# Macaron block with mixture-of-experts and attention: maxima and results turned through DRAM, first norm in two parts

## The chip, the cores and the metric

The kernel runs on one core of a Trainium2 chip. The metric is the time of one execution on the device, in microseconds (us). One core has TensorE (PE; the weight loads are shown apart as PEld), VectorE (DVE), ScalarE (ACT), GpSimd (POOL) and SyncE (SP), each with a queue of its own, and 16 DMA engines that are fed from such queues.

## What is computed

x has 4 sequences of 1024 tokens of 128 numbers, in float32. The layer is a half-weighted expert network, attention, and the same expert network again:

```python
x = x + 0.5 * ffn(layernorm(x), W1, b1, W2, b2, Wr, br)
x = x + attn(layernorm(x), Wq, bq, Wk, bk, Wv, bv, Wo, bo)
x = x + 0.5 * ffn(layernorm(x), W1, b1, W2, b2, Wr, br)

def ffn(x, ...):
    indices = argmax(softmax(x @ Wr + br))
    for i in range(8):
        xi = x * (indices == i)
        out = out + (relu(xi @ W1[i] + b1[i]) @ W2[i] + b2[i])

def attn(x, ...):
    q, k, v = (x @ W + b, split into 16 heads of 8 numbers)
    scores = einsum('bhsd,bhtd->bhst', q, k) / sqrt(8)
    return merge(einsum('bhst,bhtd->bhsd', softmax(scores), v)) @ Wo + bo
```

A token that is not expert i's still gets relu(b1[i]) @ W2[i] + b2[i] from it. These rows are the same for all tokens; the kernel calls them idle and adds their sum to the one expert's result.

## The kernel before

The tokens are 32 tiles of 128, in 8 quads of 4 tiles. There are three stages, and each block of engine programs ends with all engines meeting.

**Routing** (`route`, L253 to L482) normalises x, turns it, takes the logits, finds each token's place among the tokens sorted by expert, and writes a list of source rows. `Norm` makes statistics (L63, L74), a root on ScalarE (L83), scales on VectorE (L77, L89 to L97) and applies them (L102). In the first routing, `Setup` also loads all inputs, fills constant rows of the attention's buffers with memsets on GpSimd (L182 to L187), takes the idle rows with 64 products (L203), and sums them up on VectorE (`vector_idle` L225, `vector_rest` L233 to L237, the latter called from `list_items`, ahead of L711). The marks (L378, L380) and the columns (L382) are one-hot matrices from which TensorE makes the list (L461).

**The experts** (`Tiles`, L485 to L768) gather sorted rows with indirect DMAs on GpSimd (L559), run 39 items of a tile and an expert, and scatter the result (L566).

**Attention** (`attention`) begins with a prologue that normalises, projects, and splits q and k into three bf16 parts, stored in DRAM (L924, L936) and read back as rows (`load_heads`, L906 to L911). It goes by 16 groups of 4 heads of one batch. A group has 32 maxima units in two halves of 16. A unit is two pairs of products of queries with keys in the bank pair `ps_m` (L1071) and a maximum on VectorE (L1287). Softmax takes the row's maximum away inside the score product: two guard rows of q2 hold its negative, split into two bf16 parts, and so must be there before the half's scores. A group has 16 steps; a step has four score products (L1114), four exponentials on ScalarE (L1269), and the value products (L1125, eight records a step), whose weights have columns of ones, so that the sums come out beside the results. Those of half a group collect in one bank `ps_o`, which ScalarE copies to `oT` (`take_out`, L1190).

The order of the units is written out in `schedule`, and each takes the next of the two bank pairs of `ps_m` (`slot_of`):

```python
pair = [("max", u) for u in range(AHEAD + 2 * s, AHEAD + 2 * s + 2) if u < GROUPS * P1_UNITS]
head, tail = pair, []
if k == 3 and g:
    head, tail = pair[0:1] + [("o", g - 1)], pair[1:2]
if (s + 4) % KT == 0 and (s + 4) // KT < HALVES:
    head, tail = [("m", (s + 4) // KT)] + pair[0:1], pair[1:2]
```

TensorE does a step's head units, three scores, its tail unit, the value products of the step before and the fourth score; VectorE does its part of the units in the same order. Four kinds of unit are not maxima. An `m` unit turns a half's combined maxima (L1295) on TensorE (L1077), ScalarE and VectorE split them (L1196, L1305), and SP places them with eight DMAs (`place_guard`, L986). An `o` unit turns a group's results with 8 transposes (L1083); VectorE inverts the sums (L1312) and multiplies (L1314). For a quad of results, a `c` unit turns the gathered rows (L949, L1099, L1330) and a `y` unit multiplies by Wo (L1105); VectorE adds bo and x (L1338, L1341). Six quads (`MERGED`) are done in the last steps, two behind them (`FINISH`), while VectorE applies the second routing's norm to the six. SP's queue, in order, has the prologue's stores, the first guards ahead of the last two stores, a wait for all stores, group 1's loads, and then by group: loads for the group after next, guards of the odd half, guards of the next group's first half.

## Time and profile before

| | us |
|---|---|
| median of 3 runs (lowest to highest) | 1068.44 (1066.82 to 1069.05) |
| the profiled execution | 1066.93 |
| its span, first to last instruction | 1065.0 |
| TensorE busy, share of the span | 943.2, 89% |
| VectorE busy | 857.1, 80% |
| ScalarE busy | 741.8, 70% |
| GpSimd busy | 182.3, 17% |

The times are of the whole program. The profile is of one execution, whose time is 1.93 us longer than its span. A share of busy time is an average over the stages; matmuls are pipelined, so that a busy TensorE is not TensorE at its peak. The mean granted clock of TensorE was 0.953 of full speed.

### The profile page before, as it was taken

Reading aid. Unit: us, or ns where it says so; the run is one execution under the profiler, and the core shown is the slowest. Engines: PE = TensorE matmul, PEld = TensorE weight load, DVE = VectorE, ACT = ScalarE, POOL = GpSimd, SP = SyncE. Lnnn points to the kernel's source line nnn. Section 1 sums busy time; section 2 is a strip of 40 time slices with the busy share of each in tenths; the row PEclk is TensorE's granted clock in tenths of the full one; section 3 lists DMA queues with packets and bytes.
Section 4 is the critical chain, followed back from the end, with each engine's and each line's share of the span. In section 5 each row is a group of like instructions: output and inputs, shape, how many; then the busy total and the mean of one; then the engine's idle time right before and its main releaser. Section 6 shows DMA issues by size and latency. Waiting matters only on the chain. (4 is left out here: it accounts for less than half of the span.)

```text
span 1065.0 us, 18032 instructions
## 1 busy us (share of the span) xinstructions
PE 943.2 (89%) x6037; PEld 389.0 (37%) x6037; DVE 857.1 (80%) x1459; ACT 741.8 (70%) x1493; POOL 182.3 (17%) x198
## 2 busy tenths in 40 slices
PE   0769956779999999999999999999999999953996
PEld 0569942312222222222222222222222223442996
DVE  6876668958888888888888888888888886568664
ACT  0147726758878788787887878878788787821774
POOL 7077623700000000000000000000000000002775
PEclk9969978989999999999999999999999999965999
DMA  8533136731120202202022020220202000032321
GB/s 269 162 90 90 45 108 225 243 99 32 46 45 1 46 1 46 45 1 46 1 46 46 2 45 1 46 45 1 45 2 46 1 2 1 1 112 73 107 68 41
DMA packets 60945, 63.20 MB, mean 59 GB/s; under 512 B 8152, under 2 KB 46968, under 8 KB 60856
## 3 DMA queue, kind: packets, MB, share of 16 engines
q1 hardware_dynamic: 54152, 48.53, 17.0%
q0 software_dynamic: 5120, 12.59, 3.9%
q8 instruction: 51, 0.84, 0.3%
q10 hardware_dynamic: 1584, 0.93, 0.3%
q14 instruction: 38, 0.31, 0.1%
HBM read 36.59 MB, written 25.17 MB: 58 GB/s over the span
## 5 line engine op out<-in xcount | busy, mean ns | idle before, releaser
L1269 ACT ACTIVATE probs<-ps_s 128x512 f32<-128x512 f32 x1024 | 556.3, 600 | 144.3 <-PE ps_s L1114 118.6
L1287 DVE TENSOR_REDUCE maxima<-ps_m 128x2 f32<-128x1024 f32 x512 | 600.7, 1217 | 60.6 <-PE ps_m L1071 59.9
L1114 PE MATMUL ps_s<-q,k 74*128 74x512 bf16 (+1 forms) x1024 | 313.2, 387 | 1.3 <-ACT probs L1269 1.2
L1125 PE MATMUL ps_o<-probs,vs 128*32 128x512 f32 x2048 | 273.9, 607 | 0.7 <-ACT probs L1269 0.7
L1114 PEld LDWEIGHTS ps_s<-q,k 74*128 74x128 bf16 (+1 forms) x1024 | 81.3, 97 | 310.7 <-ACT probs L1269 230.3
L1071 PE MATMUL ps_m<-k,q 64*128 64x512 bf16 x1024 | 172.7, 387 | 21.4 <-DVE maxima L1287 12.2
L1035 POOL COPY vs<-v_and_ctx 128x256 f32<-128x256 f32 x16 | 6.3, 400 | 583.2 <-PE ps_o L1125 583.2
L1071 PEld LDWEIGHTS ps_m<-k,q 64*128 64x128 bf16 x1024 | 46.6, 93 | 138.0 <-issue 57.6
L604 PE MATMUL ps_y<-W,hT 128*128 x624 | 83.5, 277 | 0.0
L559 POOL DMA_INDIRECT v_and_ctx<-token_rows,source_i x64 | 62.3, 974 | 112.5 <-POOLq L300 93.7
L1125 PEld LDWEIGHTS ps_o<-probs,vs 128*32 128x32 f32 x2048 | 40.4, 108 | 100.7 <-issue 75.1
L604 PEld LDWEIGHTS ps_y<-W,hT 128*128 128x128 f32 x624 | 76.7, 194 | 0.4 <-issue 0.4
L633 ACT ACTIVATE xsT<-ps_x 128x128 f32<-128x128 f32 x64 | 17.7, 277 | 74.7 <-PE ps_x L583 74.6
L642 ACT ACTIVATE w1s<-W 128x644 f32 x78 | 57.8, 743 | 5.8 <-DVE by_delta L711 4.8
L649 ACT ACTIVATE hT<-ps_ha,w1s 128x128 f32<-128x128 f32 x156 | 48.4, 365 | 10.0 <-PE ps_hb L592 10.0
L592 PE MATMUL ps_ha<-xsT,w1s 128*128 (+1 forms) x312 | 50.2, 285 | 4.4 <-ACT w1s L642 4.4
L751 DVE TENSOR_SCALAR hT<-ps_hb,w1s 128x128 f32<-128x128 f32 x156 | 47.6, 347 | 5.7 <-PE ps_hb L592 1.6
L592 PE MATMUL ps_hb<-xsT,w1s 128*128 (+1 forms) x312 | 49.2, 282 | 0.0
L592 PEld LDWEIGHTS ps_ha<-xsT,w1s 128*128 128x128 f32 x312 | 43.2, 200 | 5.0 <-issue 5.0
L763 DVE SCALAR_TENSOR_TENSOR v_and_ctx<-y_sum,half_mask,v_and_ctx 128x128 f32 x78 | 27.4, 352 | 20.7 <-DVE y_sum L758 20.7
L592 PEld LDWEIGHTS ps_hb<-xsT,w1s 128*128 128x128 f32 x312 | 42.8, 199 | 0.0
L758 DVE TENSOR_TENSOR y_sum<-ps_y,w1s 128x128 f32<-128x128 f32 x78 | 22.8, 292 | 24.8 <-PE ps_y L604 24.8
(171 smaller groups left out, 590.1 us busy)
## 6 DMA issues: line engine op xcount, KB each, us to landing
k_rows<-parts SPq DMA_DIRECT2D x24, 384.0 KB, 3.7
q<-q_parts SPq DMA_DIRECT2D x75, 96.0 KB
k<-k_rows SPq DMA_DIRECT2D x15, 288.0 KB
token_rows<-x SPq DMA_DIRECT2D x16, 256.0 KB, 4.0
token_rows<-v_and_ctx SPq DMA_DIRECT2D x16, 256.0 KB, 3.8
q<-mpart SPq DMA_DIRECT2D x256, 1.0 KB
k<-k_rows SPq DMA_DIRECT2D x15, 256.0 KB
q_parts<-parts SPq DMA_DIRECT2D x8, 384.0 KB, 3.5
```

The costliest lines, as they stand in the source:

```text
L559: nc.gpsimd.indirect_dma_start(self.xs[:, t, :], None, self.dram["token_rows"], bass.IndirectOffsetOnAxis(ap=self.routes.source_i[:, t:t + ...
L592: last = nc.tensor.matmul(self.ps_h[c // 2][i % 2][:, (c % 2) * P:(c % 2 + 1) * P], self.w1s[:, i % W_ROTATION, c * P:(c + 1) * P], self.x ...
L604: last = nc.tensor.matmul(self.ps_y[i % 2][:, 0:D], self.hT[:, i % 2, c * P:(c + 1) * P], w["W2"][:, bass.ds(e, 1), c, :].rearrange("p a d ...
L642: nc.scalar.activation(self.w1s[:, i % W_ROTATION, :], w["W1"][:, bass.ds(e, 1), :].rearrange("p a h -> p (a h)"), ACT.Copy).then_inc(self ...
L649: last = nc.scalar.activation(self.hT[:, i % 2, c * P:(c + 1) * P], self.ps_h[0][i % 2][:, c * P:(c + 1) * P], ACT.Relu, bias=self.w1s[:, ...
L751: last = nc.vector.tensor_scalar(self.hT[:, i % 2, c * P:(c + 1) * P], self.ps_h[1][i % 2][:, (c - 2) * P:(c - 1) * P], self.w1s[:, i % W_ ...
L763: nc.vector.scalar_tensor_tensor(out=row, in0=self.y_sum[:, i % 2, :], scalar=self.half_mask[:, i:i + 1], in1=row, op0=ALU.mult, op1=ALU.a ...
L1071: last = nc.tensor.matmul(ps_m[slot][:, j % 2, :], q2[buffer(g)][rows, j, qt * P:(qt + 1) * P], k2[buffer(g)][rows, j, kh * HALF:(kh + 1) ...
L1114: nc.tensor.matmul(ps_s[n % 3][:, :], k2[buffer(g)][0:contracted, j, kt * P:(kt + 1) * P], q2[buffer(g)][0:contracted, j, u * HALF:(u + 1) ...
L1125: last = nc.tensor.matmul(ps_o[32 * j:32 * (j + 1), :], vs[buffer(g)][:, kt, j, :], probs[:, s % 2, j, :], start=(kt == 0), stop=(kt == KT ...
L1269: nc.scalar.activation(probs[:, s % 2, j, :], ps_s[n % 3][:, :], ACT.Exp, scale=SCALE).then_inc(exped, 1)
L1287: nc.vector.tensor_reduce(maxima[:, :, pr, qt, kh], ps_m[slot][:, :, :], AX.X, ALU.max).then_inc(unit_free[slot], 1)
```

## The change

- **Maxima.** The `m` units are gone. VectorE combines a half's maxima as before; GpSimd splits them with three small operations (`split_maxima`); VectorE turns them in blocks of 32 x 32 (`turn_maxima`), one or two units later; SP stores them to DRAM (`guards`), waits, and reads them back as guard rows with two DMAs.
- **Results.** The `o` and `c` units are gone. SP stores each half group's `oT` in DRAM (`sums`), waits, and reads results and sums back in the layout in which TensorE takes them for Wo (`results`). VectorE inverts the sums of half a batch at once, 128 x 512 (`invert`), at the steps in `DIVIDED` (60, 71, 124, 135, 188, 199, 252; the eighth behind the last step); GpSimd multiplies (`multiply`; VectorE for the last). GpSimd adds bo to x early on (`add_bias`), and the `y` units only add to x. Seven quads are merged instead of six.
- **The end of the attention.** ScalarE and SP send the last results' rows straight from `oT` with four small DMAs each. ScalarE applies the norm to two of the seven quads, VectorE to five.
- **Loads.** Group 1's loads go out before the stores of quads 6 and 7, with the first guards behind them. The first loads of group 0 go out before the stores of quad 1, and the statistics and scales of the prologue's norm are spread among other work.
- **The first routing.** Its norm goes in two parts of four quads; ScalarE applies quads 0, 1, 4 and 6. Half of the marks goes to ScalarE, half to GpSimd (both routings). The idle rows are copied by ScalarE and summed on GpSimd (`add_up`, `gpsimd_rest`), and `RESTED` is waited for there.

```diff
-    def vector_idle(self, dve):
-        dve.wait_ge(self.idle_done, 1)
-        self.nc.vector.tensor_copy(self.idle[:, :, :], self.ps_idle[:, :, :]).then_inc(self.dve_step, 1)
...
+    def scalar_idle(self, act):
+        act.wait_ge(self.idle_done, 1)
+        self.nc.scalar.activation(self.idle[:, :, :], self.ps_idle[:, :, :], ACT.Copy).then_inc(self.idle_out, 1)
...
+    def add_up(self, pool, rows, out, before):
+
+        nc, tree, half = self.nc, self.tree, EXPERTS // 2
+        wait_unless_zero(pool, self.rest_step, before)
+        nc.gpsimd.tensor_tensor(tree[:, :, :], rows[:, 0:half, :], rows[:, half:, :], ALU.add).then_inc(self.rest_step, 1)
+        pool.wait_ge(self.rest_step, before + 1)
+        nc.gpsimd.tensor_tensor(tree[:, 0:2, :], tree[:, 0:2, :], tree[:, 2:4, :], ALU.add).then_inc(self.rest_step, 1)
+        pool.wait_ge(self.rest_step, before + 2)
+        nc.gpsimd.tensor_tensor(out[:, :], tree[:, 0, :], tree[:, 1, :], ALU.add).then_inc(self.rest_step, 1)
+
+    def gpsimd_biases(self, pool):
+
...
+    def gpsimd_rest(self, pool):
 
...
+        pool.wait_ge(self.idle_out, 1)
+        self.add_up(pool, self.idle, self.total, 3)
+        pool.wait_ge(self.rest_step, 6)
+        nc.gpsimd.tensor_tensor(self.total[:, :], self.total[:, :], self.biases[:, :], ALU.add).then_inc(self.rest_step, 1)
+        pool.wait_ge(self.rest_step, 7)
+        half = EXPERTS // 2
...
-                for q in range(ready, QUADS):
+                def statistics(q):
...
-                    last = norm.statistics(quad_tiles(q))
-                last.then_inc(vstep, 1)
-                norm.spread(dve, late)
-                norm.refine(dve, late)
-                for q in range(ready, QUADS):
-                    norm.apply(quad_tiles(q))
...
+                    norm.refine(dve, (span.start, span.stop), n)
+                    nc.vector.scalar_tensor_tensor(out=shift[:, span], in0=mv[:, span, 0], scalar=-1.0, in1=rt[:, 6, span],
+                                                   op0=ALU.mult, op1=ALU.mult).then_inc(shifted, 1)
+
+                for n, (first_quad, end_quad) in enumerate(spans):
+                    for q in range(first_quad + (n > 0), end_quad):
+                        last = statistics(q)
+                    last.then_inc(vstep, 1)
+                    norm.spread(dve, (first_quad * QUAD, end_quad * QUAD), n)
+                    if n + 1 < len(spans):
+                        statistics(end_quad)
+                    scales(n)
+                    for q in range(first_quad, end_quad):
+                        if q not in by_act:
+                            norm.apply(quad_tiles(q))
...
-                dve.wait_ge(routed, 22)
-                nc.vector.tensor_tensor(marks[:, :, 0, :], hot[:, :, :],
-                                        w["iota_b"][:, 0:TILES].unsqueeze(2).to_broadcast([P, TILES, TILES]), ALU.mult)
-                nc.vector.tensor_scalar(marks[:, :, 1, :], hot[:, :, :], w["partition"][:, 0:1], None, ALU.mult)
+                dve.wait_ge(routed, 21)
...
                     setup.gpsimd_fill(pool)
+                    setup.gpsimd_biases(pool)
+                pool.wait_ge(routed, 22)
+                nc.gpsimd.tensor_tensor(marks[:, :, 0, :], hot[:, :, :],
+                                        w["iota_b"][:, 0:TILES].unsqueeze(2).to_broadcast([P, TILES, TILES]), ALU.mult).then_inc(marked, 1)
...
+                def normalise(q):
+                    act.wait_ge(shifted, 1 if q < QUAD else 2)
+                    for t in quad_tiles(q):
+                        last = nc.scalar.activation(xn_sb[:, t, :], x_sb[:, t, :], ACT.Identity, bias=shift[:, t:t + 1], scale=rt[:, 6, t:t + 1])
...
+                act.wait_ge(routed, 22)
+                nc.scalar.activation(marks[:, :, 1, :], hot[:, :, :], ACT.Copy, scale=w["partition"][:, 0:1]).then_inc(marked, 1)
+                if setup:
...
+MERGED = 7
+OUTPUT_STEP = (243, 245, 247, 249, 251, 252, 254)
...
-    merged = {SOFT - 2 * MERGED - (n == 0) * 2 + n: [(("c", "y")[n % 2], n // 2)] for n in range(2 * MERGED)}
+    merged = {s: [("y", q)] for q, s in enumerate(OUTPUT_STEP)}
...
-        steps.append((head + merged.get(s, []), tail))
+        steps.append([("max", u) for u in range(AHEAD + 2 * s, AHEAD + 2 * s + 2) if u < GROUPS * P1_UNITS] + merged.get(s, []))
...
+
+    at = {}
+    for q in range(MERGED):
+        b, u = divmod(q, 2)
...
+        def last_results(engine, target, first):
+
+            engine.wait_ge(o_out, 2 * GROUPS)
+            for j in range(GH):
+                row = (GPB - 1) * GH * DK + j * DK
+                engine.dma_start(target[row:row + DK, :], oT[32 * j + first:32 * j + first + DK, 1, :]).then_inc(o_in[1], 16)
...
                 def place_guard(h):
...
+                    sp.wait_ge(turned_maxima, h + 1)
+                    sp.dma_start(dram["guards"][h, :, :].rearrange("c (a r) -> a c r", r=32), blocks[h % 2][:, :]).then_inc(guards_out, 16)
+                    sp.wait_ge(guards_out, 16 * (h + 1))
...
+                    for j in range(2):
+                        sp.dma_start(q2[buffer(g)][guard(j):guard(j) + GUARDS, j::2, u * HALF:(u + 1) * HALF], rows[j, :, :, :]).then_inc(in_m[buffer(g)], 16)
...
+                def results(g, u):
...
+                    sp.wait_ge(o_out, 2 * g + u + 1)
+                    sp.dma_start(dram["sums"][g, u, :, :], oT[:, u, :]).then_inc(o_stored[u], 16)
+                    sp.wait_ge(o_stored[u], 16 * (g + 1))
+                    if g % GPB == 0 and b:
+                        sp.wait_ge(divided, 2 * b - 1 + u)
+                    sp.dma_start(ctxT[rows, tokens], sums[:, 0:DK, :]).then_inc(o_in[u], 16)
+                    sp.dma_start(den[rows, u, :], sums[:, DK:2 * DK, :]).then_inc(o_in[u], 16)
...
                 store(0)
-                store_key(sp, 1, 0)
-                store_query(sp, 1)
                 first_load(0)
-                store_key(sp, 1, 1)
-                store_key(sp, 1, 2)
+                store(1)
                 first_load(1)
-                for q in range(FIRST, QUADS - 2):
+                for q in range(FIRST, QUADS):
+                    if q == QUADS - 2:
+                        place_guard(0)
                     store(q)
-                place_guard(0)
-                for q in range(QUADS - 2, QUADS):
-                    store(q)
+                    if q == QUADS - 3:
+                        load(1)
                 for p in range(2):
                     sp.wait_ge(parts_stored[p], 16 * STORES * (QUADS // 2))
-                load(1)
                 for g in range(GROUPS):
                     if 1 <= g < GROUPS - 2:
                         sp.wait_ge(step_done, STEPS * g)
                         load(g + 2)
+                    if g:
+                        results(g - 1, 1)
                     place_guard(2 * g + 1)
                     if g == 0:
                         load(2)
+                    results(g, 0)
                     if g + 1 < GROUPS:
                         place_guard(2 * g + 2)
+                last_results(sp, ctxT[:, (QUADS - 1) * HALF:], 0)
                 for p in range(BUFS):
-                    sp.wait_ge(in_m[p], 16 * 2 * GH * GUARDS * ((GROUPS - 1 - p) // BUFS + 1))
+                    sp.wait_ge(in_m[p], 16 * 2 * 2 * ((GROUPS - 1 - p) // BUFS + 1))
+                for u in range(2):
+                    sp.wait_ge(o_in[u], O_IN * GROUPS + (2 * GH * 16 - O_IN if u else 0))
...
+                def split_maxima(h):
+
+                    pool.wait_ge(combined, h + 1)
+                    wait_unless_zero(pool, turned_maxima, h)
+                    nc.gpsimd.tensor_scalar(split[:, :, 0, :], top[:, :, :], -1.0, None, ALU.mult).then_inc(split_step, 1)
+                    nc.gpsimd.tensor_scalar(negated[:, :, :], top[:, :, :], -1.0, None, ALU.mult).then_inc(split_step, 1)
+                    pool.wait_ge(split_step, 3 * h + 2)
+                    nc.gpsimd.tensor_tensor(split[:, :, 1, :], negated[:, :, :], split[:, :, 0, :], ALU.subtract).then_inc(split_step, 1)
...
+                def multiply(q):
+
+                    pool.wait_ge(recip, q + 1)
+                    columns = ctxT[:, q * HALF:(q + 1) * HALF]
+                    nc.gpsimd.tensor_tensor(columns, columns, den[:, q % 2, :], ALU.mult).then_inc(divided, 1)
...
-                for q in range(MERGED):
-                    gather_rows(pool, nc.gpsimd.tensor_copy, q)
+                split_maxima(1)
+                for q in range(QUADS):
+                    add_bias(q)
+                split_maxima(2)
+                for g in range(1, GROUPS):
+                    if g < GROUPS - 2:
+                        pool.wait_ge(step_done, STEPS * g)
+                        stage(g + 2)
+                    if g % GPB == 0:
+                        split_maxima(2 * g + 1)
+                        multiply(2 * (g // GPB) - 1)
+                    else:
+                        split_maxima(2 * g + 1)
+                    if g + 1 < GROUPS:
+                        split_maxima(2 * g + 2)
+                    if g % GPB == GPB - 1:
+                        multiply(2 * (g // GPB))
 
             @block.tensor
...
+                    wait_unless_zero(act, o_stored[u], 16 * g)
...
-                    gather_rows(act, nc.scalar.copy, q)
+                last_results(act, den[:, 1, :], DK)
+                act.wait_ge(shifted_2, 1)
+                for t in range(BY_DVE, MERGED * QUAD):
+                    last = nc.scalar.activation(xn_next[:, t, :], w["x"][:, t, :], ACT.Identity, bias=shift[:, t:t + 1], scale=rt[:, 6, t:t + 1])
+                last.then_inc(normed_2, 1)
 
...
-
-                def split_unit(h, slot, used):
-
-                    dve.wait_ge(unit_full[slot], used + 1)
...
-                    nc.vector.tensor_tensor(ctx_sb[:, g, :, :].rearrange("p t (j d) -> p t j d", d=DK),
-                                            src[:, :, :, 0:DK], rden[:, :, :, :].to_broadcast([P, KT, GH, DK]),
-                                            ALU.mult).then_inc(unit_free[slot], 1)
+                    nc.vector.tensor_reduce(top[:, :, :].rearrange("p a (i t) -> p a i t", t=QUAD), maxima[:, :, :, u:u + QUAD, :],
+                                            AX.X, ALU.max).then_inc(combined, 1)
+
+                def turn_maxima(h):
+
+                    dve.wait_ge(split_step, 3 * h + 3)
+                    if h >= 2:
+                        dve.wait_ge(guards_out, 16 * (h - 1))
+                    nc.vector.transpose(blocks[h % 2][:, :], split[:, :, :, :].rearrange("p a r c -> p (a r c)")).then_inc(turned_maxima, 1)
+
+                def invert(q):
+
+                    b, u = divmod(q, 2)
+                    dve.wait_ge(o_in[u], O_IN * GPB * (b + 1) + (2 * GH * 16 - O_IN if q == QUADS - 1 else 0))
+                    nc.vector.reciprocal(den[:, u, :], den[:, u, :]).then_inc(recip, 1)
...
+                    nc.vector.tensor_tensor(w["x"][:, tiles_of, :], ps_m[slot][:, 0, :].rearrange("p (t d) -> p t d", d=D), w["x"][:, tiles_of, :],
+                                            ALU.add).then_inc(unit_free[slot], 1)
                     if q < MERGED:
-                        dve.wait_ge(residual, q + 1)
+                        dve.wait_ge(unit_free[slot], used + 1)
...
+                norm_2.apply(range(BEFORE_LAST))
+                invert(QUADS - 1)
+                dve.wait_ge(recip, QUADS)
+                columns = ctxT[:, (QUADS - 1) * HALF:]
+                nc.vector.tensor_tensor(columns, columns, den[:, 1, :], ALU.mult).then_inc(divided, 1)
+                norm_2.apply(range(BEFORE_LAST, BY_DVE))
+                for unit in FINISH:
                     do_unit(*unit)
-                for q in range(len(FINISH) - 1, MERGED):
-                    norm_2.apply(quad_tiles(q))
+
 
```

## Rows read from the trace of the kernel before

**Rows 1.** Busy time by stage (stretch, length, engines with instructions, clock, DMA share, GB/s)

```profile
267.20:888.40 621.20, 613.87 (x3725) 157.97 (x3724) 545.88 (x533) 501.37 (x953) 5.92 (x14) 1.00 0.12 26
...
888.40:930.30 41.90, 39.96 (x271) 16.77 (x270) 24.03 (x70) 32.90 (x62) 2.45 (x4) 1.00 0.01 1
...
930.30:947.10 16.80, 7.12 (x36) 5.88 (x32) 12.49 (x44) 3.24 (x5) 0.00 (x0) 0.59 0.00 0
```

**Rows 2.** Timeline of TensorE in one group (start, us, line, instructions merged)

```profile
400.30 1.06 PE L1125 MATMUL ps_o<-probs,vs 128*32 128x512 f32 x8
...
402.92 1.07 PE L1125 MATMUL ps_o<-probs,vs 128*32 128x512 f32 x8
...
406.56 1.06 PE L1125 MATMUL ps_o<-probs,vs 128*32 128x512 f32 x8
...
409.48 1.06 PE L1125 MATMUL ps_o<-probs,vs 128*32 128x512 f32 x8
...
411.43 0.39 PE L1071 MATMUL ps_m<-k,q 64*128 64x512 bf16 x2 [0.23 <-DVE maxima L1287]
...
412.50 1.06 PE L1125 MATMUL ps_o<-probs,vs 128*32 128x512 f32 x8
```

**Rows 3.** Timeline of VectorE in the same stretch (in brackets: idle before, and what ended it)

```profile
402.05 2.36 DVE L1287 TENSOR_REDUCE maxima<-ps_m 128x2 f32<-128x1024 f32 x2 [0.27 <-PE ps_m L1071]
...
408.83 0.28 DVE L1305 SCALAR_TENSOR_TENSOR mpart<-ps_m,mpart 16x128 bf16<-16x128 f32 x1 [0.93 <-ACT mpart L1196]
```

**Rows 4.** Timeline of TensorE at the start of the softmax

```profile
218.94 1.06 PE L1125 MATMUL ps_o<-probs,vs 128*32 128x512 f32 x8
...
225.62 1.04 PE L1071 MATMUL ps_m<-k,q 64*128 64x512 bf16 x4 [5.29 <-DMA q<-q_parts]
...
231.99 1.07 PE L1125 MATMUL ps_o<-probs,vs 128*32 128x512 f32 x8
```

**Rows 5.** Groups by line and shape, VectorE (count, busy us, mean ns, idle before)

```profile
L89 DVE RECIPROCAL rt_a<-rt_a 128x4 f32<-128x4 f32 x2 | 0.4, 178 | 0.8 <-ACT rt_a L83 0.8
...
L89 DVE RECIPROCAL rt_a<-rt_a 128x24 f32<-128x24 f32 x1 | 0.3, 291 | 0.0
...
L89 DVE RECIPROCAL rt<-rt 128x32 f32<-128x32 f32 x1 | 0.4, 355 | 0.3 <-ACT rt L83 0.3
...
L1341 DVE TENSOR_TENSOR x<-x,plus_bo 128x512 f32<-128x512 f32 x8 | 5.5, 692 | 0.3
...
L77 DVE TENSOR_SCALAR rt_a<-mv_a 128x24 f32<-128x24 f32 x1 | 0.2, 178 | 0.0
```

**Rows 6.** Timeline of SP's queue

```profile
200.05 5.74 SPq L986 DMA_DIRECT2D q<-mpart  x8
...
398.80 0.31 SPq L906 DMA_DIRECT2D k<-k_rows  x1
...
402.87 0.30 SPq L911 DMA_DIRECT2D q<-q_parts  x1
```

**Rows 7.** DMA issues (count, KB each, median us from issue to landing)

```profile
token_rows<-x SPq DMA_DIRECT2D x16, 256.0 KB, 4.0
...
b_rows<-L_ffn_b SPq DMA_DIRECT2D x1, 16.0 KB, 1.8
```

**Rows 8.** Groups by line and shape, GpSimd

```profile
L959 POOL TENSOR_TENSOR probs<-probs,parts 128x512 f32<-128x512 f32 x12 | 13.7, 1154 | 30.1 <-ACT parts L1218 30.1
```

**Rows 9.** Timeline of VectorE and GpSimd in the first norm

```profile
19.12 1.80 POOL L183 MEMSET k<- 64x2048 bf16 x1
...
19.47 1.49 DVE L77 TENSOR_SCALAR rt<-mv 128x32 f32<-128x32 f32 x1
...
20.98 1.80 POOL L185 MEMSET q<- 64x2048 bf16 x1
...
22.09 0.72 DVE L95 TENSOR_SCALAR rt<-rt 128x32 f32<-128x32 f32 x1
```

**Rows 10.** Timeline of ScalarE at the first weights

```profile
62.95 0.74 ACT L642 ACTIVATE w1s<-W 128x644 f32 x1 [4.45 <-DVE by_delta L711]
```

255 lines of the change are left out of this document (111 added, 144 removed).

## The prediction

> **What bounds the kernel now.** I read the busy time by stage first [rows 1]. The softmax stage from 267.2 to 888.4 is 621.2 us long, with TensorE busy for 613.87 of it, VectorE for 545.88 and ScalarE for 501.37; the granted clock is 1.00, the 2.4 GHz level. So TensorE's queue sets the pace there, and VectorE is not far behind. The timeline of TensorE [rows 2] shows how. The starts of the value products (L1125) mark the steps. A plain step is 402.92 - 400.30 = 2.62 us. The step with the turn of the results (L1083) takes 406.56 - 402.92 = 3.64, so that unit costs 1.02. The steps on which a turn of the maxima (L1077) bears take 409.48 - 406.56 = 2.92 and 412.50 - 409.48 = 3.02, so that unit costs 0.30 + 0.40 = 0.70; the second part is the stop at 411.43, where TensorE waits for VectorE, which had stood 0.93 us behind ScalarE's part of the split [rows 3]. VectorE in a plain step has 0.27 us to spare. Early on, a stop of 5.29 us waits for group 1's loads [rows 4]. Outside the softmax, the routing stages and the turn between softmax and routing are chains of small dependent pieces.
>
> **Softmax, units taken out.** The pattern stands in all sixteen groups. Between 267.2 and 888.4 and in the group before, 30 turns of maxima and 14 turns of results go (the last of each falls into the end, below): 30 x 0.70 + 14 x 1.02 = 35.3 us less on TensorE, which no other engine hides. The work put in their place is on GpSimd (three small operations a half), SP (three DMAs a half instead of eight, and three more for the results) and VectorE (one 32-column transpose a half, near 0.2 us as the reciprocal and other 32-column rows are). GpSimd is idle there, and the transpose fits into VectorE's 0.27 us: I cost both at nothing. If that cover were gone, the transposes would be worth 31 x 0.2 = 6 us.
>
> **Softmax, the new reciprocals.** Before, a reciprocal had 32 columns. Now eight have 512 columns of 128 partitions, and six of them stand between maxima in VectorE's queue (steps 60, 71, 124, 135, 188, 199). The trace has 178 ns for 4 columns and 355 for 32 [rows 5]: 6.3 ns a column, so 178 + 508 x 6.3 = 3.4 us. From below, it might go like an addition of the same shape, 0.69 us [rows 5]; from above, the slope between 24 and 32 columns is 8.0 ns, which would make it 4.2 us. I take 3.4, as the rows are of this very operation and the longer distance smooths them. Behind it the maxima wait, behind them TensorE, which has two banks for them: it loses 3.4 less the spare 0.27, 3.1 us, six times: +18.6. 
>
> **The early stall.** From 218.94 to 231.99 two steps take 13.05 us [rows 4]; without the wait they would take 2 x 2.62 + 0.30 = 5.54. Group 1's loads now go out before the last two stores, 5 us or more earlier than needed: -7.5. They are put ahead of the first guard rows on SP, though. Before, these went out at 200.05 [rows 6] and nothing waited for them. Now SP sends ten loads first (398.80 to 403.17 in a later group, 4.4 us [rows 6]), then a store to DRAM, a wait for it, and two loads. A small transfer lands in 1.8 us, one of 256 KB in 4.0 [rows 7]. So: 200 + 4.4 + 0.5 + 2.5 + 0.7 + 2.0 = 210.1, and TensorE's first unit of the softmax, at 209.7 before, comes out at 210.4: +0.7. The first norm's rearrangement in this block wins some 2 us on VectorE ahead of that (statistics put into its waits, the first maxima begin earlier), and the guard wait eats them. Bounds: -2 and +4.
>
> **The end of the softmax.** From 888.4 to 930.3 [rows 1] seven y units stand where six pairs of c and y, one o and one m stood. That wins about 1.6 us, but the seventh reciprocal (step 252) is followed by a multiplication on GpSimd (1.15 us for this shape [rows 8]) and the y unit at step 254: 3.4 + 1.2 after VectorE comes to it, about 2.3 us too late for TensorE. Net +0.7, bounds -2 and +4.
>
> **The tail.** It is 16.8 us long now [rows 1], a chain through all engines. The new one: 0.6 for the copy out of the bank, four DMA issues 1.8, landing 2.0, reciprocal 3.4, multiplication 0.7, Wo at the low clock 2.1, addition 0.7, and gaps, 11.7 in all; the norm of the other tiles runs beside it. -5.1.
>
> **The first routing.** The clue is here [rows 9]. A VectorE scale operation on 32 columns (L77) took 1.49 us and ended at 20.96, as the memset begun at 19.12 for 1.80 us had just ended; L95 took 0.72 and ended at 22.81, as the memset begun at 20.98 had ended. L77 on 24 columns takes 178 ns [rows 5]. So such operations stand still while GpSimd works. The change moves the norm of quads 0 to 3 into the time of the memsets, which last until 23.8 us. Ten such operations there (two of the scales, eight applications) get through only at the memsets' ends, one or two at each, so the last of them ends between 21 and 24 us, and the statistics of quads 5 to 7 (2.6 us), which are queued behind them, then their scales (3.3) and ScalarE's eight applications (3.2, at 0.4 each) end at 30 to 33 us, where VectorE had ended all at 31.6; ScalarE's copies then stand behind its applications, 6 us to the logits where it was 4.3. So splitting the norm, which without the blocking would bring the logits 4.5 us forward, brings nothing; I take +1.0. Then the marks on GpSimd (1024 columns, 2.3 us by [rows 8]) and the rest of the sums (5.2 us) meet the 32 column operations (5.3 us), which are of the same blocked kind and now wait where they ran back to back; the block can't end before GpSimd's sums, which follow TensorE's 64 products and ScalarE's copy of them: another +4. Against that, VectorE's sums ahead of the first weights go (ScalarE waits 4.45 us for them [rows 10]), and with their gaps the first products start 4.6 us sooner after the block: -4.6. Sum +0.4; bounds -8.2 (nothing is blocked) and +6. The Trainium skill (SBUF — State Buffer, SBUF: two separate sides) calls the port pair that VectorE and GpSimd share an exclusive lock, held for the full instruction. By that rule, this part of the change is hurt as above; the trace agrees, with its 1.49 us. In the second routing, a norm of four tiles instead of eight wins 0.8 and the marks on GpSimd lose 0.8: nothing.
>
> **New waits.** VectorE waits for GpSimd's split before each transpose, with maxima behind it; two units (2.4 us) lie between, so it is hidden but for the first, 1 to 1.5 us, in the prologue (within the bounds there). SP waits for each store of sums and of guards; behind it are the next loads. For an odd half: the loads are issued 2.9 us after the group's first value product, the sums land behind them at 8.9 (0.4 + 4.0 and 1.6 for the loads still moving), their reads are issued by 9.9, the guards' two trips end at 15.1 (0.4 + 2.0 + 0.8 + 2.0), and TensorE needs them at 17.1, 1.2 ahead of seven plain steps. ScalarE's wait for the sums stored a group before is long met.
>
> **The sum** is against the profiled execution, 1066.9 us: -35.3 + 18.6 - 7.5 + 0.7 + 0.7 - 5.1 + 0.4 = -27.5, so 1039.4. The median of the runs is 1.5 above that execution: 1040.9.
>
> **Rivals.** (1) GpSimd and VectorE don't block each other as the first routing supposes, because the loser gets in between two operations cheaply. For it: a GpSimd memset began 20 ns after L77 ended, unharmed. Against: 1.49 and 0.72 us. Then first routing -8.2 instead of +0.4, second -2.4 instead of 0: 1029.9. Chance 0.2. (2) The long reciprocal costs like an addition. Six times 2.7, 2.7 in the tail and 2.3 in the end less: 1019.7. Chance 0.08. (3) The early stall doesn't go, as the loads still land behind the stores, or guards take its place: 1048.4. Chance 0.1. (4) Slower: the guard rows come late in each odd half. Their way now has two trips through DRAM in a row behind the sums. If each trip takes the 4.0 us of the larger stores instead of 2.0 [rows 7], the 4.0 more less the 2.0 to spare leave 2.0 late, and 2.7 with 0.7 of issue time: 15 groups x 2.7 = 40 us, 1081. It decides from about 1.8 us a group on. Against it: the guards are 8 KB. Chance 0.1. The forecast's own case has 0.5, and 0.02 is for a stall that just cancels the gain.
>
> **Numbers.** The range takes in cases 1, 2 and 3 and the bounds of the main one (1028 to 1056, the reciprocal of 4.2 us, 6 us more, among them): 1018 to 1057, leaving out rival 4 and a little more. A measurement of this kernel can tell about 0.2% from no change. Faster by more than that has 0.9, within it 0.02, slower 0.08.
>
> **What would show it.** Right: plain steps still of 2.62 us in all places where L1083 and L1077 stood; six gaps of 3 us in the steps behind the reciprocals, each of them 3.4 us long; the stop at group 1's loads gone; scale operations of the first norm lasting to the ends of memsets; the block behind the softmax over some 12 us after the last value product. Wrong: TensorE waits for guard rows at the half's first step, or reciprocals under 1 us, or logits of the first routing well before 35 us.

## The result, and the profile after

The changed kernel takes 1057.61 us (median of 5 runs, 1053.53 to 1058.40), the kernel before 1067.74 us beside it: a ratio of 0.9896 with the 95% interval 0.9884 to 0.9909, so 10 us or 1% faster. The forecast was 1040.9 us with a range up to 1057: the sign was right, and the gain was 10 us where 27.5 were forecast. The profiled execution has a span of 1055.5 us against 1065.0.

The page of the changed kernel, its busy times and the row of the granted clock:

```profile
span 1055.5 us, 17569 instructions
PE 912.6 (86%) x5771; PEld 371.6 (35%) x5845; DVE 857.0 (81%) x1397; ACT 747.9 (71%) x1488; POOL 230.9 (22%) x314
PEclk9779978979999988999999899999989999965999
```

TensorE's busy time is 30.6 us less than before (943.2 there). Part of that is a gap in the page: it has records of 950 score products where the kernel makes 1024. The run with the short memsets (below), whose softmax is the same and whose page has all 1024, shows 925.9 us. The span is only 9.5 us shorter. The clock row shows where to look: single digits of 8 stand in the middle of the softmax, where the clock was 1.00 throughout before [rows 1]. The same stages as in [rows 1], now:

```profile
core 0: us, PE busy (x) PEld busy (x) DVE busy (x) ACT busy (x) POOL busy (x), PEclk, DMA share, GB/s
263.10:881.00 617.90, 592.64 (x3521) 147.15 (x3584) 554.43 (x511) 497.38 (x925) 31.41 (x102) 0.97 0.18 44
881.00:923.40 42.40, 37.40 (x241) 13.92 (x245) 20.46 (x71) 33.28 (x62) 1.94 (x4) 1.00 0.06 20
923.40:936.40 13.00, 2.08 (x12) 1.78 (x8) 11.12 (x29) 4.11 (x11) 0.00 (x0) 0.56 0.05 11
```

The long stage is hardly shorter, TensorE is busy for 25 us less than its length (7 before), and its mean clock is 0.97. Of the 25 us, 15.2 are twelve waits for VectorE's maxima. Another 6.9 are 27 small gaps that the page with all records doesn't show, so they are most likely missing records. I divided the softmax into its sixteen groups, by the starts of the value products (L1216 now, sixteen steps a group). Before, a group took 44.38 us and the first one 51.16. Now the eight groups from 1 to 14 without a long reciprocal take 41.97 us each and the first 42.46, but the six with one take 47.52, 47.37, 46.34, 47.30, 46.34 and 47.26. One of these places in TensorE's timeline:

```profile
start us, us, engine line op out<-in xcount [idle before <-releaser]
379.56 0.39 PE L1205 MATMUL ps_s<-q,k 128*128 128x512 bf16 x1
381.82 0.39 PE L1184 MATMUL ps_m<-k,q 64*128 64x512 bf16 x2 [1.87 <-DVE maxima L1367]
382.94 0.61 PE L1184 MATMUL ps_m<-k,q 64*128 64x512 bf16 x2 [0.73 <-DVE maxima L1367]
383.48 1.46 PE L1205 MATMUL ps_s<-q,k 74*128 74x512 bf16 x3
384.88 1.94 PE L1216 MATMUL ps_o<-probs,vs 128*32 128x512 f32 x8
```

VectorE's queue and the granted clock over the same stretch:

```profile
375.07 2.36 DVE L1367 TENSOR_REDUCE maxima<-ps_m 128x2 f32<-128x1024 f32 x2 [0.15 <-PE ps_m L1184]
377.34 3.34 DVE L1397 RECIPROCAL den<-den 128x512 f32<-128x512 f32 x1
380.60 4.55 DVE L1367 TENSOR_REDUCE maxima<-ps_m 128x2 f32<-128x1024 f32 x4
387.94 2.36 DVE L1367 TENSOR_REDUCE maxima<-ps_m 128x2 f32<-128x1024 f32 x2 [2.79 <-PE ps_m L1184]
```

```profile
380.00:382.00 2.00, 0.18 (x2) 0.10 (x2) 2.00 (x3) 0.58 (x1) 1.24 (x1) 1.00 0.00 0
382.00:384.00 2.00, 1.26 (x6) 0.35 (x5) 2.00 (x3) 0.00 (x0) 0.02 (x1) 0.54 0.00 0
384.00:386.00 2.00, 2.00 (x11) 0.24 (x9) 1.15 (x2) 1.57 (x3) 0.00 (x0) 0.50 0.00 0
386.00:388.00 2.00, 2.00 (x9) 0.24 (x5) 0.07 (x1) 0.60 (x1) 0.00 (x0) 0.50 0.00 0
388.00:390.00 2.00, 1.81 (x12) 0.44 (x11) 2.00 (x2) 1.04 (x3) 0.00 (x0) 0.75 0.00 0
390.00:392.00 2.00, 2.00 (x16) 0.45 (x13) 1.18 (x2) 1.15 (x4) 0.00 (x0) 1.00 0.00 0
```

The reciprocal has the length that was forecast, 3.34 us. TensorE stops behind it for 1.87 and 0.73 us (waits for VectorE's maxima). Then comes what the forecast has no term for: the granted clock is 0.50, the 1.2 GHz level, from 382 to about 389 us. Eight value products take 1.94 us, three score products 1.46; at the full clock they take 1.07 and 0.83 (as in the run with two pieces, below). At the end VectorE, far behind before, stands idle for 2.79 us: TensorE is now the late one, through its clock alone.

The six places are of two kinds. At the four whose groups take 47.3 to 47.5 us, the granted clock is at 0.50 for about 7 us, as here. At the two of 46.34 us it is there for about 3.5 us only:

```profile
563.00:566.50 3.50, 3.50 (x15) 0.43 (x8) 1.75 (x2) 1.74 (x4) 0.00 (x0) 0.51 0.00 0
```

The softmax also starts 4.7 us later than before (first value product at 220.7, before at 216.0), though both kernels enter the attention's first turn at 151.3. SP's queue, and TensorE's wait at the end of it, a stretch that answers to [rows 6]:

```profile
199.69 1.11 SPq L974 DMA_DIRECT2D k<-k_rows  x1
...
205.51 0.61 SPq L1049 DMA_DIRECT2D guards<-blocks  x1
211.33 1.32 SPq L1053 DMA_DIRECT2D q<-guards  x2
```

```profile
205.59 1.16 PE L1239 MATMUL ps_o<-Wv,xnT_a 128*128 128x128 f32 x8
214.19 1.04 PE L1184 MATMUL ps_m<-k,q 64*128 64x512 bf16 x4 [7.44 <-issue]
```

SP sends group 1's ten loads first; the store of the guard rows is issued at 205.51 and their two reads only at 211.33. TensorE needs them and stands idle for 7.44 us (the profile names no releaser; by the kernel the semaphore waited for there is that of these reads).

### The profile page after: what moved, and what is told of

Read it like the earlier page. It is cut to its first block and busy times, and to the rows that moved or that the text cites. A ratio compares the mean times of both kernels' runs of the same rounds, so it can differ in the third digit from the quotient of the medians.

```text
span 1055.5 us, 17569 instructions
## 1 busy us (share of the span) xinstructions
PE 912.6 (86%) x5771; PEld 371.6 (35%) x5845; DVE 857.0 (81%) x1397; ACT 747.9 (71%) x1488; POOL 230.9 (22%) x314
## 3 DMA queue, kind: packets, MB, share of 16 engines
q1 hardware_dynamic: 63472, 61.05, 20.9%
## 5 line engine op out<-in xcount | busy, mean ns | idle before, releaser
L1205 PE MATMUL ps_s<-q,k 74*128 74x512 bf16 (+1 forms) x950 | 300.3, 392 | 5.2 <-ACT probs L1348 2.7
L1216 PE MATMUL ps_o<-probs,vs 128*32 128x512 f32 x2048 | 278.2, 616 | 0.7 <-ACT probs L1348 0.7
L1184 PE MATMUL ps_m<-k,q 64*128 64x512 bf16 x1024 | 165.8, 396 | 36.2 <-DVE maxima L1367 19.8
L1123 POOL TENSOR_SCALAR split<-top 128x16 bf16<-128x16 f32 x32 | 8.1, 253 | 386.1 <-DVE top L1383 371.0
L1216 PEld LDWEIGHTS ps_o<-probs,vs 128*32 128x32 f32 x2048 | 40.5, 108 | 110.8 <-issue 96.2
L621 POOL DMA_INDIRECT v_and_ctx<-token_rows,source_i x64 | 61.5, 961 | 29.5 <-issue 18.6
L811 DVE TENSOR_SCALAR hT<-ps_hb,w1s 128x128 f32<-128x128 f32 x156 | 47.5, 346 | 5.8 <-PE ps_hb L654 2.8
```

The source lines that it names most:

```text
L621: nc.gpsimd.indirect_dma_start(self.xs[:, t, :], None, self.dram["token_rows"], bass.IndirectOffsetOnAxis(ap=self.routes.source_i[:, t:t + ...
L811: last = nc.vector.tensor_scalar(self.hT[:, i % 2, c * P:(c + 1) * P], self.ps_h[1][i % 2][:, (c - 2) * P:(c - 1) * P], self.w1s[:, i % W_ ...
L1184: last = nc.tensor.matmul(ps_m[slot][:, j % 2, :], q2[buffer(g)][rows, j, qt * P:(qt + 1) * P], k2[buffer(g)][rows, j, kh * HALF:(kh + 1) ...
L1205: nc.tensor.matmul(ps_s[n % 3][:, :], k2[buffer(g)][0:contracted, j, kt * P:(kt + 1) * P], q2[buffer(g)][0:contracted, j, u * HALF:(u + 1) ...
L1216: last = nc.tensor.matmul(ps_o[32 * j:32 * (j + 1), :], vs[buffer(g)][:, kt, j, :], probs[:, s % 2, j, :], start=(kt == 0), stop=(kt == KT ...
```

## The experiments

All ratios are against the kernel before, run beside each; times of the changed kernel are its 1057.6 us. Edits are shown shortened. Two theories to begin with. **C**: a long stop of TensorE costs its length and, behind it, products at the 1.2 GHz level. **L**: a reciprocal costs its length alone, and the rest comes from what was added around it.

**The long reciprocals, cut short.** The other columns are left uninverted in both runs, so their results are not those of the layer; the runs measure time alone.

```
-nc.vector.reciprocal(den[:, u, :], den[:, u, :])
+columns = slice(0, HALF if q >= MERGED - 1 else 32)      # second run: 256
+nc.vector.reciprocal(den[:, u, columns], den[:, u, columns])
```

> The changed kernel, with the six reciprocals in the middle of the softmax (steps 60, 71, 124, 135, 188, 199) cut from 512 to 32 columns; the rest of those sums isn't inverted, so this is left out of the computation. Theory C (clock): each costs 5.4 to 5.5 us now, 3.1 for TensorE's stop and over 2 for the products at the 1.2 GHz level that follow a stop; with short ones both go, groups 3, 4, 7, 8, 11 and 12 take 42.0 us like the others, and the kernel about 30 us less than the changed one (1027 to 1028 us). Theory L (length): what a reciprocal costs is its own length less 0.27 us, 18.6 us for six, and the other 12 us come from what is added around it (GpSimd's multiplications, the reads of the sums), which stay: 1039 us, groups of about 44 us.

> The same six reciprocals cut to 256 of 512 columns (the other half of those sums isn't inverted). Length: 1.70 us each by 3.34 for 512, so a stop of 1.4 us. If the clock falls only after a stop of over 3 us, each group with one takes 42.0 + 1.4 = 43.4 us and the kernel about 22 us less than the changed one (1036 us). If it falls after 1.4 us too, each costs about 3 to 3.5 us, the groups take 45 and the kernel is at 1046 us. Theory L: 1.65 less for each of six than in the changed kernel, 10 us in all, 1048 us.

With 32 columns: 1029.92 us, ratio 0.9642 (0.9626 to 0.9658). The groups 1 to 14 take 41.95 to 42.16 us, all of them. The six reciprocals thus cost nearly what C says, 30 us in the groups (5.05 each; C had 5.4 to 5.5). 27.7 reach the total: the last group takes 44.00 us instead of 41.36, since behind the stop of 2.00 us at its last y unit, which both kernels have, the clock falls here and not there. GpSimd's multiplications and the transfers are all still there and cost next to nothing, so L falls.

With 256 columns: 1036.18 us, ratio 0.9700 (0.9684 to 0.9716). The groups take 43.20 to 43.22 us, 1.24 above a plain one, and TensorE's timeline has one stop of 0.73 or 0.74 us in each. The granted clock stays at the 2.4 GHz level:

```profile
378.00:390.00 12.00, 10.99 (x69) 2.70 (x68) 10.98 (x10) 8.72 (x17) 1.67 (x2) 1.00 0.01 1
```

Half the columns cost 1.24 us, all of them 5.05 on average, four times as much. A piece of 256 takes 1.74 us, so VectorE had 1.74 - 1.24 = 0.50 us to spare. By that a whole one, of 3.34, should cost 2.84.

**The same columns in two pieces.** The sharpest test of C: nothing is left out.

```
 first = STEPS * (GPB * b + GPB - 1) + (12 if u == 0 else STEPS + 7)
-at[first] = q
+for n in range(PIECES):     # 2; at q == MERGED - 1 still one
+    at[first + n] = (q, n * HALF // PIECES, (n + 1) * HALF // PIECES)
```

> The changed kernel, with each of the six long reciprocals as two of 256 columns, one step apart; all 512 columns are inverted. In the run with 256 columns alone one such piece stopped TensorE for 0.73 us, cost 1.24 us and left the granted clock at 1.00. If the clock falls with the length of a single stop, two of them cost 2 x 1.3 = 2.5 us for each reciprocal, groups with one take 44.5 us, none shows products at the 1.2 GHz level, and the kernel takes about 15 to 17 us less than the changed one (1041 to 1043 us). Rival: the two stops close together count like one, the clock falls as before, the groups take 46 to 47 us and the kernel 1052 to 1058 us.

Measured: 1042.82 us, ratio 0.9773 (0.9756 to 0.9789), groups of 44.42 to 44.44 us, so 2.47 for each reciprocal. In TensorE's timeline, with the clock under it:

```profile
380.55 0.39 PE L1190 MATMUL ps_m<-k,q 64*128 64x512 bf16 x2 [0.27 <-DVE maxima L1373]
381.67 0.39 PE L1190 MATMUL ps_m<-k,q 64*128 64x512 bf16 x2 [0.73 <-DVE maxima L1373]
381.99 0.83 PE L1211 MATMUL ps_s<-q,k 74*128 74x512 bf16 x3
382.75 1.07 PE L1222 MATMUL ps_o<-probs,vs 128*32 128x512 f32 x8
...
384.41 0.39 PE L1190 MATMUL ps_m<-k,q 64*128 64x512 bf16 x2 [0.27 <-DVE maxima L1373]
385.54 0.39 PE L1190 MATMUL ps_m<-k,q 64*128 64x512 bf16 x2 [0.74 <-DVE maxima L1373]
```

```profile
376.00:392.00 16.00, 13.93 (x85) 3.34 (x88) 15.12 (x13) 11.45 (x22) 1.67 (x2) 1.00 0.04 6
```

TensorE stops twice for 0.27 + 0.73 us, and all products keep their length. The same work, done in one piece, costs twice as much. Of the 2.58 us between 5.05 and 2.47, 0.36 go because VectorE's 0.50 us to spare is used twice; the other 2.2 are the clock. By the same measure the 30.3 us of the six whole reciprocals are 17.0 of stops (six times 2.83, which a trace below shows) and 13.3 of low clock.

**Eight pieces.** With `PIECES = 8`, and GpSimd's multiplications behind the next split so that it never waits in front of one:

> The whole reciprocal, but in eight pieces of 64 columns, one a step, behind the two maxima of each; GpSimd's multiplications are moved behind the next split. A piece takes about 0.48 us, 0.2 more than VectorE has to spare in a step. Theory C: TensorE never stops, the granted clock stays at 1.00 in groups 3, 4, 7, 8, 11 and 12, each reciprocal costs 8 x 0.2 = 1.7 us instead of 5.5, and the kernel takes 30 - 10 = 20 us less than the changed one, 1037 us. Theory L: the same 1.7 us for the pieces instead of 3.1, 8 us less than the changed kernel, 1049 us.

1032.83 us, ratio 0.9668 (0.9651 to 0.9684), better than expected. A piece takes 539 ns:

```profile
L1402 DVE RECIPROCAL den<-den 128x64 f32<-128x64 f32 x48 | 25.9, 539 | 0.0
```

The steps with a piece take 2.66 instead of 2.62 us, and only where the transpose of the maxima falls into one as well, 2.94 and 2.76. The pair of groups 3 and 4 takes 42.13 + 43.16, which is 1.35 us for two reciprocals where they cost 10.95 before. The 0.04 us a step is 0.54 less the 0.50 to spare, as above. I had expected 1.7 us for a reciprocal, by the 0.27 us of [rows 3]. That is the only gap in a plain step. The rest of the 0.50 lies in the listed lengths, which overlap: a piece and the two maxima behind it are listed with 0.54 and 2.29 us, but what follows each begins 0.46 and 2.20 us after it, 2.66 in all:

```profile
381.46 0.54 DVE L1402 RECIPROCAL den<-den 128x64 f32<-128x64 f32 x1
381.92 2.29 DVE L1372 TENSOR_REDUCE maxima<-ps_m 128x2 f32<-128x1024 f32 x2
384.12 0.54 DVE L1402 RECIPROCAL den<-den 128x64 f32<-128x64 f32 x1
```

So eight pieces win for two reasons. TensorE has no stop behind which the clock falls, and VectorE's spare time of eight steps is used instead of one step's.

**Guard rows first.**

```
-if q == QUADS - 2:
-    place_guard(0)
 store(q)
 if q == QUADS - 3:
+    place_guard(0)
     load(1)
```

> On SP the guard rows of the first half go out ahead of group 1's ten loads instead of behind them. If the 5.8 us that the trip to DRAM took there came from the loads queued ahead of it, the trip takes 2 to 2.5 us, TensorE's first value product of the softmax starts at 214 to 216 us instead of 220.7, and the kernel gains 4 to 6 us (1052 to 1053 us). Rival: a trip of guard rows takes that long by itself at this point, with the loads of the group ahead gone or not: first product at 217 to 221 us. Second rival: group 1's loads come late again, and a stop of 1 to 5 us stands in steps 2 to 4; then nothing is gained in all.

1050.74 us, ratio 0.9839 (0.9822 to 0.9855), 6.9 us less than the changed kernel. The traced execution is the fastest of the four, 1046.2 us; most of what it has beyond the 6.9 is in the groups with a reciprocal, as shown below. SP's queue and TensorE's:

```profile
199.28 0.61 SPq L1049 DMA_DIRECT2D guards<-blocks  x1
202.99 1.32 SPq L1053 DMA_DIRECT2D q<-guards  x2
204.36 0.42 SPq L974 DMA_DIRECT2D k<-k_rows  x1
```

```profile
207.31 1.03 PE L1183 MATMUL ps_m<-k,q 64*128 64x512 bf16 x4 [1.43 <-DVE v_and_ctx L1423]
```

The trip to DRAM, from the start of the store to the issue of the reads, takes 3.7 us instead of 5.8, and it starts 6.2 us sooner (0.9 of these come from the stages before, which were that much quicker in this execution). TensorE no longer waits for guard rows but for VectorE, 1.43 us. The first value product is at 213.8. The interval behind it is 4.16 us instead of 3.11, since the clock is at the lower level there, so 1 us is given back; no stop for group 1's loads is left. By the two traces the edit itself is thus worth 5 us: 6.9 at the first value product, less 0.9 and 1.0.

The same trace holds a control for C. In its group 7 TensorE stops for 1.67 and 0.73 us behind the reciprocal, but the clock does not fall; in group 8, after 1.87 and 0.74, it does. The windows of both:

```profile
552.00:556.00 4.00, 2.75 (x16) 0.66 (x16) 3.84 (x4) 1.55 (x3) 0.72 (x1) 1.00 0.00 0
...
584.00:590.00 6.00, 5.07 (x21) 0.96 (x22) 3.84 (x5) 2.17 (x4) 0.40 (x1) 0.72 0.18 66
```

Group 7 takes 44.79 us, 2.83 more than a plain one, group 8 takes 46.34, 4.38 more. In the changed kernel's trace group 7 has the same stops, 1.67 and 0.74 us, but the clock falls and it takes 46.34. So the stop alone costs 2.83, the 2.84 worked out above from the other run, and the clock 1.5 on top of it, up to 2.7 elsewhere (47.52). How often and for how long the clock falls differs between executions. That is also the likely reason why the changed kernel's runs lie 4.9 us apart (1053.53 to 1058.40) while those of the one with eight pieces lie within 1.3. The mean granted clock of each run fits: 0.944 in the changed kernel's two fastest, 0.932 to 0.937 in its other three, 0.951 or 0.952 in all four with eight pieces. There are traces of one run each, so where the clock fell in the others was not seen.

**GpSimd's memsets.** k and q are filled as pairs of 16-bit elements, so half as many:

```
-self.nc.gpsimd.memset(self.k2[p][64:96, 0::2, :], 1.0)
+self.nc.gpsimd.memset(self.k2[p][64:96, 0::2, :].bitcast(F32), TWO_ONES)
```

> The changed kernel, with GpSimd's nine memsets of k and q written as 32-bit elements, half as many: by the vs memset (1024 elements of 32 bits, 0.96 us) they take 0.96 instead of 1.80 us each, so the last ends near 15.5 us instead of 23.8. Theory B (VectorE's small operations stand still during GpSimd's): the eight scale operations of the first quads then run at 0.26 us each instead of 6.45 us for eight, and the logits come 3 to 4 us sooner (34 to 35 us for 37.9). Rival: the first norm is late through something else (waits, the table load, TensorE's low clock) and the logits stay at 37 to 38 us. Of the 3 us, little reaches the end if TensorE's clock rises at the same point of time as before, the 3 us if it rises the sooner: total 1054 to 1058 us.

1053.54 us (1049.75 to 1057.86), ratio 0.9862 (0.9818 to 0.9906). The total has so wide an interval that it says little alone; the marks in the trace say more. The logits come at 34.3 us (37.9), the last expert product ends at 136.7 (140.3), the attention's first turn starts at 147.8 (151.3) and the first value product is at 216.8 (220.7). A mark of one execution is itself uncertain. Six traced kernels have the changed kernel's code up to the experts' end (changed, 32 and 256 columns, two and eight pieces, guard rows first), and their logits come from 36.2 to 38.4 us, their last expert product ends from 139.3 to 141.4. The three with this run's code there (this one and the two of the last section) have 32.6 to 34.4 and 136.5 to 138.3. The gain is thus real, but 3.6 us is the size in one pair of traces. Rows of the changed kernel, then of this run, in [rows 9]'s view:

```profile
14.56 6.45 DVE L102 TENSOR_SCALAR v_and_ctx<-x,mv,rt 128x128 f32<-128x128 f32 x8
```

```profile
13.49 4.31 DVE L103 TENSOR_SCALAR v_and_ctx<-x,mv,rt 128x128 f32<-128x128 f32 x8
```

The memsets end at 16.2 us here (23.8). The eight applications take 4.31 us instead of 6.45. By the expectation it would be 2.1, but the last memsets and the first addition of the bias sums (16.43) still stand beside them. The second eight, with nothing on GpSimd, take 2.13 us in the changed kernel. It is the TENSOR_SCALAR rows that are long beside GpSimd's work; sixteen aggregations (BATCH_NORM_AGGREGATE) take 1.17 us beside a memset in the changed kernel (at 10.28), and 1.17 with nothing on GpSimd in this run (at 20.16). So the blocking is real, and the amount of GpSimd's work in that time bears on when the logits come.

**The norm in one part again**, with the slow and with the short memsets:

```
-by_act = (0, 1, QUAD, QUAD + 2) if setup else ()
-spans = ((0, QUAD), (QUAD, QUADS)) if setup else ((ready, QUADS),)
+by_act, spans = (), ((ready, QUADS),)
```

> The changed kernel, with the first norm in one part on VectorE again, as before; marks and bias sums stay on GpSimd, the memsets stay slow. Theory B (with the slow memsets the split brings nothing, the statistics of the later quads wait behind eight blocked operations): the logits come at 35.5 to 37 us for 37.9 of the changed kernel, that is 1 to 2 us sooner, and the total is the same within 2 us. Rival: the split brings what it was sized at without blocking, 4.5 us, and the logits come at 41 us or later.

> The same, with the memsets as 32-bit elements: beside the run with the norm in two parts and such memsets (logits at 34.3 us) it tells what the split is worth when nothing blocks. By the prediction's working 4.5 us, so 38 to 39 us here; but the kernel before, with blocked scales worth 2 us, had them at 35.9, so by that row 34 to 35 us: then the split is worth under 1 us even without blocking.

Logits at 37.7 us with the slow memsets (37.9 with the split), total 1056.61; at 35.0 with the short ones (34.3 with the split), total 1050.95, ratio 0.9861 (0.9835 to 0.9888). So the split is worth -0.2 us with the blocking and 0.7 without it by these traces, and both are within the 2.2 us by which executions of one code differ. What they do rule out is the 4.5 us that I had given it without blocking. The first run was expected at 35.5 to 37 and came out later. Its row says why:

```profile
23.15 10.29 DVE L102 TENSOR_SCALAR v_and_ctx<-x,mv,rt 128x128 f32<-128x128 f32 x32
```

In the kernel before the same 32 took 8.54 us from 23.07 on. What stands beside them now are the bias sums on GpSimd, from 23.85 to 26.5 (L235 to L239). That makes 1.75 us. It is the likely reason why the logits of the changed kernel are 2 us late, and not the split norm. The next run, with the split and without bias sums on GpSimd, has its logits at 36.5 us, which agrees, but neither is clear of the spread of 36.2 to 38.4.

**Marks and sums back on VectorE** in the first routing, as in the kernel before (its `vector_idle`, `vector_rest` and the two operations that make the marks):

```
+nc.vector.tensor_tensor(marks[:, :, 0, :], hot, iota_b, ALU.mult)      # was GpSimd
+nc.vector.tensor_scalar(marks[:, :, 1, :], hot, partition, None, ALU.mult)   # was ScalarE
...
+    self.setup.vector_rest(dve)      # in list_items; was gpsimd_rest
```

> The changed kernel, with this part undone in the first routing: both marks, the copy of the idle sums and the bias sums are on VectorE again, as in the kernel before, while the first norm stays in two parts. Theory B: the 32 column operations run back to back again (5.3 us instead of 11.1), the block's end comes 3 to 4 us sooner (55 to 56 us for 59.2), and the first weights wait again for the sums (4.5 us), so the first products start within 1 us of the changed kernel's 65.4; the total is the same within 2 us. Rival: the part brings a real gain or loss of 3 us or more at the experts' end (140.3 us in both kernels).

1056.87 us, ratio 0.9897 (0.9878 to 0.9915), so no difference. The columns:

```profile
47.44 5.29 DVE L439 TENSOR_SCALAR columns<-iota_b,in_tile 128x128 bf16<-128x128 bf16 x32
```

In the changed kernel the 32 take 11.07 us, from 46.99 to 58.06. Here the block ends at 54.4 instead of 59.2 us, a little sooner than expected, and the first products start at 64.65 instead of 65.37. By the fourth item even that is gone; its products start at 71.50 in the kernel before, 71.51 in the changed one, 71.50 here, though they started at 63.83, 65.37 and 64.65. The granted clock is why. From 68 to 70 us it is 0.52 in the kernel before, which had started first, and 0.96 in the changed one. What decides when it rises is open. That all three meet at 71.50 is partly luck: in the six executions of one code the fourth item starts from 70.6 to 72.6 us.

**Together, and with another tail.**

```
 for i in range(QUAD):                      # the last two reciprocals in 4 pieces
+    invert(QUADS - 1, i * P, (i + 1) * P)
+    ... multiply these 128 columns; TensorE waits for each quarter alone
-last_results(sp, values); last_results(act, sums)
+last_results(sp, (2, 3), (0, 1, 2)); last_results(act, (0, 1), (3,))   # sums first, then values
-BY_DVE, BEFORE_LAST = 5 * QUAD, 3 * QUAD
+BY_DVE = BEFORE_LAST = 3 * QUAD
```

> Three of the edits together: the long reciprocals in eight pieces, the first half's guard rows ahead of group 1's loads, GpSimd's memsets as 32-bit elements. If they add up: 25 us (pieces) + 6 us (guards) + 0 to 3 us below the changed kernel's 1057.6, 1024 to 1027 us. If they meet in one place, 1028 to 1033 us.

> The same, and the tail rearranged: the last sums' four transfers are issued by two queues, two each, ahead of those of the values (the last one lands 1.5 us sooner); the last two reciprocals go in four pieces of 128 columns, each followed by its multiplication and its own quarter of the output product, so that the products run beside the next piece; ScalarE normalises 16 tiles instead of 8. Expected from the rows of the tail: last y unit 0.9 us less of waiting at step 254, block end 2.6 us sooner after the last value product (11.4 us instead of 14.0), in all 3 to 3.5 us below best1. Rival: ScalarE, with sixteen tiles to normalise, or the transfer of the values becomes the last to end, and under 1 us is left.

The three edits add up: 1023.59 us, ratio 0.9584 (0.9555 to 0.9614), 34.0 less than the changed kernel, where their own gains are 24.8 + 6.9 + 4.1 = 35.8. With the tail 1017.97 us, ratio 0.9532 (0.9514 to 0.9550), the fastest of all and 5.6 below the one without. The products of the last output unit in the changed kernel, and here:

```profile
933.62 2.04 PE L1196 MATMUL ps_m<-Wo,v_and_ctx 128*128 128x128 f32 x8 [10.19 <-DVE v_and_ctx L1504]
```

```profile
891.59 0.77 PE L1206 MATMUL ps_m<-Wo,v_and_ctx 128*128 128x128 f32 x2 [6.36 <-DVE v_and_ctx L1523]
...
895.06 0.80 PE L1206 MATMUL ps_m<-Wo,v_and_ctx 128*128 128x128 f32 x2 [0.40 <-DVE v_and_ctx L1523]
```

From the start of the last value products (922.37 and 884.16) to the end of the last addition (936.39 and 896.59) it takes 12.4 instead of 14.0 us, 1.6 won of the 2.6 expected; the last sixteen steps take 39.87 instead of 41.36, 1.5 won of 0.9 expected. These 3.1 us are as expected in sum. The other 2.5 of the 5.6 lie ahead of the softmax, where nothing was changed (the logits come at 32.6 for 34.4), and are a difference between the two executions.

## Why the prediction was wrong

By its own terms, each against the spans of the two profiled executions:

| term | forecast | measured |
|---|---|---|
| units out of TensorE's queue, and the early stall | -35.3 - 7.5 | -42.4 |
| six long reciprocals | +18.6 | +30.3 |
| first routing and start of the softmax | +0.4 + 0.7 | 0.0 + 4.7 |
| end of the softmax | +0.7 | +0.5 |
| tail, to the block's end | -5.1 | -3.8 |
| second routing and experts | 0 | +1.2 (within the spread) |
| sum | -27.5 | -9.5 |

**Units and early stall: right.** A plain step is 2.62 us everywhere, as foretold. The transposes take 0.20 us each and are hidden, as priced (though the reciprocal of 32 columns, named beside them, has 0.355 in [rows 5]). Groups 1 to 14 without the reciprocals' share: 14 x (44.38 - 41.97) = 33.7, and the first group 51.16 - 42.46 = 8.7.

**Reciprocals: the step that failed.** I wrote that TensorE "loses 3.4 less the spare 0.27, 3.1 us, six times". The length was right to 0.1 us, 3.34, by the rows of 4 and 32 columns. The term that was missing is what follows the stop: products at the 1.2 GHz level for 3.5 to 7 us, 1.5 to 2.7 us more each, 13.3 us in all. The run with two pieces shows it, with the same columns and half the loss. And the rows were there to be read. In the kernel before, the stop of 5.29 us ([rows 4]) is followed by four L1071 products of 1.04 us in all, and then:

```profile
226.59 1.46 PE L1114 MATMUL ps_s<-q,k 74*128 74x512 bf16 x3
227.98 1.93 PE L1125 MATMUL ps_o<-probs,vs 128*32 128x512 f32 x8
```

The forecast even had the price in a sum: it gave the early stall 7.5 us where the stop is 5.29, so some 2.2 us were what followed. It did not ask why, and left that term out behind the new stops. Of the miss of 18 us, 11.7 are this: 13.3 for the clock, less 1.6 since a stop costs 2.83 and not 3.1.

**The start of the softmax: right in kind, wrong in size.** The order of SP's queue was seen, and the first guard rows priced at "200 + 4.4 + 0.5 + 2.5 + 0.7 + 2.0 = 210.1". The loads took 5.8 us to issue instead of 4.4, since I took them from a later, quiet group, and the store behind them landed 5.2 us after its issue instead of 2.5 [rows 7]: it stands behind ten loads in the same queue, where the small transfer of [rows 7] is the first of its queue. TensorE came out at 214.2, beyond even the bound of +4, and at the lower clock. The run with the guard rows first shows that the order is the cause. It takes 2.1 us off the trip itself, and lets it start 5.3 us sooner.

**First routing: right in sum, partly by luck.** The blocking was as forecast: applications to 20.9 us, the block's end 5.6 us later (forecast 1.0 + 4), the first weights no longer waiting. But the logits were late more likely through the bias sums than through the split. And the 0.0 at the end was not this balance: the first products were 1.5 us later, and the clock gave that back. It is uncertain by a microsecond besides: in the six executions of one code the attention's first turn starts from 150.4 to 152.4 us, against 151.3 before. Rival 1 (no blocking) is out by the run with the short memsets. Even so, the norm's split gave 0.7 us there and not 4.5.

**Tail.** Forecast 11.7 us, it took 13.0 from the end of the last value products. The four DMA issues of the sums take 3.67 us on ScalarE instead of 1.8 (the first alone 1.53), as I had priced them by a queue that was already running:

```profile
923.76 0.58 ACT L1278 ACTIVATE oT<-ps_o 128x512 f32<-128x512 f32 x1
...
924.37 3.67 ACTq L1016 DMA_DIRECT2D den<-oT  x4
...
929.39 3.35 DVE L1397 RECIPROCAL den<-den 128x512 f32<-128x512 f32 x1 [1.00 <-DMA den<-oT]
```

**Second routing and experts.** From the block's end to the end it takes 119.1 us, 117.9 before. In the runs above, none of which changes this part, it takes 117.9 to 119.4, so the 1.2 us can't be told from the difference between executions.

Rival 2 (a cheap reciprocal) is out by 3.34 us. Rival 3 is half true: the stall at the loads went, but guard rows took a part of its place. Rival 4 (guard rows late in each odd half) did not happen: in the sixteen groups no wait for guard rows is left after the first.

## What to carry to other kernels

A stop in the engine that sets the pace is not priced by its length alone. Look in the trace for the products just behind an existing stop, and compare them with the same products elsewhere. Where one long operation has to go into a full queue, cut it into pieces, one a step: here the same 512 columns cost 5.05 us whole, 2.47 in two pieces and 0.68 in eight. And price a small transfer by a row in which it stands behind the same neighbours in the same queue.
